# A token, attention and mixture kernel: the halves of q and k spread over the partitions through DRAM instead of by 0/1 products, four hidden buffers for two, a new order for every engine

## The chip, the core and the metric

The kernel runs on one core of one Trainium2 chip. Its five engines each work through a queue of their own in order: TensorE (PE, matrix products), VectorE (DVE), ScalarE (ACT), GpSimd (POOL) and SyncE (SP, which here issues every DMA). They meet through semaphores: an instruction waits until a count is reached, and whatever stands behind it in that queue waits too. The metric is the time on the device in microseconds, lower is better. Time before: a median of 4962.4 us over 3 runs (4959.22 to 4967.59).

## The reference, cut to what matters

```python
# x: (64, 256, 80).  After a 5-tap projection: h: (64, 252, 128)
h = tok(x)                                            # taps, relu, norm over batch and time
h = h + softmax_attention(_layernorm(h))              # 8 heads of 16; a band of +0.1 on the scores
h = h + top2_mixture(_layernorm(h))                   # 8 experts of 256, gelu
h = h + linear_attention(_layernorm(h))               # 8 heads of 16, elu + 1, causal; values of 64
h = h + causal_block(_layernorm(h))                   # 2 heads of 64, then 8 experts of 512, gelu

# softmax_attention:
scores = jnp.einsum('bqhd,bkhd->bhqk', q, k) / np.sqrt(hd) + band
attn = jax.nn.softmax(scores, axis=-1)
# linear_attention:  Q = elu(x @ W_q.T) + 1,  K = elu(x @ W_k.T) + 1
# num = Q . cumsum(K V),  out = num / (Q . cumsum(K))
```

## The kernel before

The 64 sequences are taken in 32 pairs. A pair is 4 tiles of 126 positions, 504 columns (`TOK`). A first phase, up to about 165 us, does the token projection of all pairs and puts it in DRAM (`y_scratch`); the rest goes through the pairs.

To keep near float32 with 16-bit products, each operand is a high and a low half in f16 and a product is three (`mm3`, L1274 to L1276): high with high, high with low, low with high.

Each pair passes through five streams. `softmax_queries_and_keys` (letter q) makes q and k of the softmax attention; `softmax_attention` (a) is that attention and its gates; `linear_and_causal_attention` (l) is the linear attention, the causal attention and the gates of the second mixture; `hidden` (h) is one chunk of 128 hidden columns of an expert, and `output` (o) its way back. In round r the engines work at l of pair r, a of pair r+1, q of pair r+2, and 48 chunks of h and of o. A generator per stream yields its steps, and a string of letters per engine (`PE_ROUND`, `DVE_ROUND`, `ACT_ROUND`, `POOL_ROUND`, L165 to L172) says which stream's next step stands next in that engine's queue. SP has no such string before: it waits for a pair's end, stores it and loads the input of the pair four later.

A chunk of h: PE makes three products of 504 columns into PSUM (`pf`), ACT applies gelu (L838) into one of `HIDS = 2` buffers `hid`, DVE casts the high half (L1239), POOL subtracts for the low half (L615). ACT may write a `hid` buffer again only when POOL has read it. A chunk of o: PE makes 4 x 3 products of 128 columns, and DVE adds at an expert's last chunk (L1258).

The scores of a head have 16 rows for contraction. Both attentions put high and low terms of q and k under each other: 64 partitions per head hold q = (high, high, low, -) against k = (high, low, high, -), so that one product gives the three. In the softmax attention a fourth row carries minus the row maximum in q, against a 1 in k. Getting rows from `qk_hi`/`qk_lo` (128 partitions: head x 16) to the spread layout (`q_spread`, `k_spread`: four groups of two heads) is the work that the change is about. Before, PE does it by products with 0/1 matrices: `spread_queries` (L1329, L1330) and `spread_keys` (L1341, L1342), 2 products of 504 columns per group, 4 groups, for q and k and in both attentions; DVE copies the q groups out of PSUM (L942), ACT the k groups (L680, with the 1 added as a bias). Only 3 (softmax) or 2 (linear) PSUM banks are there, so PE waits for the copies in between.

## Time and profile before

| | us |
|---|---|
| median of 3 runs | 4962.4 |
| lowest, highest | 4959.22, 4967.59 |
| the profiled execution's own time | 4962.4 |
| its span, first to last instruction | 4960.7 |
| PE busy | 4458.9 (90%) |
| DVE busy | 3778.6 (76%) |
| ACT busy | 2839.1 (57%) |
| POOL busy | 2494.6 (50%) |
| mean granted TensorE clock | 0.964 |
| DMA queue of the program | 38.01 MB, 2.7% of 16 engines |

Busy time is the time in which an engine has an instruction at work. Products on PE overlap: the end of one is modelled, and the next begins before it. So a sum over busy times of PE is not the time that its queue needs; the distance between the starts of rows is. A row of the time line gives start, duration, engine, line, operation, the tile written and those read, how often it follows itself, and in brackets the idle time of the engine before it and what ended that. `pa` are the PSUM banks of the attentions, `pf` those of the mixtures.

### The profile page before, as it was taken

Reading aid. Unit: us, or ns where it says so; the run is one execution under the profiler, and the core shown is the slowest. Engines: PE = TensorE matmul, PEld = TensorE weight load, DVE = VectorE, ACT = ScalarE, POOL = GpSimd, SP = SyncE. Lnnn points to the kernel's source line nnn. Section 1 sums busy time; section 2 is a strip of 40 time slices with the busy share of each in tenths; the row PEclk is TensorE's granted clock in tenths of the full one; section 3 lists DMA queues with packets and bytes.
Section 4 is the critical chain, followed back from the end, with each engine's and each line's share of the span. In section 5 each row is a group of like instructions: output and inputs, shape, how many; then the busy total and the mean of one; then the engine's idle time right before and its main releaser. Section 6 shows DMA issues by size and latency. Waiting matters only on the chain.

```text
span 4960.7 us, 106933 instructions
## 1 busy us (share of the span) xinstructions
PE 4458.9 (90%) x42560; PEld 3182.8 (64%) x42560; DVE 3778.6 (76%) x9518; ACT 2839.1 (57%) x4601; POOL 2494.6 (50%) x2392
## 2 busy tenths in 40 slices
PE   7677999999999999999999999999999999999986
PEld 3345766666666666666766666676666666666665
DVE  3356877788877788788788778878778888777864
ACT  3224655666566656656655666565566656655643
POOL 1123555555555555555555555555555555555544
PEclk9778999999999999999999999999999999999998
DMA  4100000000000000000000000000000000000000
GB/s 144 37 3 1 6 6 6 1 6 6 5 6 6 6 1 6 5 6 6 6 6 6 2 6 6 6 6 6 6 1 6 6 6 6 6 6 4 2 3 5
DMA packets 45604, 44.86 MB, mean 9 GB/s; under 512 B 19625, under 2 KB 44081, under 8 KB 45105
## 3 DMA queue, kind: packets, MB, share of 16 engines
q1 hardware_dynamic: 45104, 38.01, 2.7%
q8 instruction: 337, 5.52, 0.5%
q14 instruction: 163, 1.33, 0.1%
HBM read 21.48 MB, written 16.52 MB: 8 GB/s over the span
## 4 chain that ended last, share of the span: by engine, by line
PE 46%; DVE 35%; ACT 9%; POOL 5%; issue 4%; DMA 1%; SPq 0%; ACTq 0%; DVEq 0%
PE pa L1562 7%; PE pf L1274 6%; PE pf L1275 6%; PE pf L1276 6%; DVE hid_hi L1239 5%; DVE xn L931 5%; DVE h L1258 4%; PE pa L1442 3%; ACT hid L838 2%; PE pa L1544 2%; PE pa L1274 2%; PE pa L1428 2%; DVE q_spread L942 2%; DVE minus_max L1037 2%; PE pa L1318 2%
## 5 line engine op out<-in xcount | busy, mean ns | idle before, releaser
L615 POOL TENSOR_TENSOR hid_lo<-hid,hid_hi 128x504 f16<-128x504 f32 x1536 | 1773.5, 1159 | 1890.6 <-DVE hid_hi L1239 1890.6
L838 ACT ACTIVATE hid<-pf,vec 128x504 f32<-128x504 f32 x1536 | 1037.4, 682 | 1103.1 <-POOL hid_lo L615 629.9
L1274 PE MATMUL pf<-w_hi,hid_hi 128*126 128x128 f16 x6144 | 1144.2, 225 | 21.8 <-DVE h L1258 21.8
L1276 PE MATMUL pf<-w_hi,hid_lo 128*126 128x128 f16 x6144 | 1133.0, 223 | 0.0
L1275 PE MATMUL pf<-w_lo,hid_hi 128*126 128x128 f16 x6144 | 1132.9, 223 | 0.0
L1239 DVE CAST hid_hi<-hid 128x504 f16<-128x504 f32 x1536 | 784.2, 517 | 276.6 <-ACT hid L838 275.7
L1274 PEld LDWEIGHTS pf<-w_hi,hid_hi 128*126 128x126 f16 x6144 | 857.0, 139 | 118.9 <-DVE h L1258 33.2
L1275 PEld LDWEIGHTS pf<-w_lo,hid_hi 128*126 128x126 f16 x6144 | 858.0, 140 | 38.4 <-issue 5.1
L1276 PEld LDWEIGHTS pf<-w_hi,hid_lo 128*126 128x126 f16 x6144 | 858.8, 140 | 0.0
L1258 DVE SCALAR_TENSOR_TENSOR h<-pf,gates,h 126x128 f32<-126x128 f32 x2048 | 573.7, 342 | 129.3 <-PE pf L1276 129.1
L1274 PE MATMUL pf<-xf_hi,w_hi 128*128 128x504 f16 x1536 | 602.4, 392 | 18.5 <-ACT hid L838 18.3
L1275 PE MATMUL pf<-xf_lo,w_hi 128*128 128x504 f16 x1536 | 598.1, 389 | 0.0
L1276 PE MATMUL pf<-xf_hi,w_lo 128*128 128x504 f16 x1536 | 596.0, 388 | 0.0
L571 POOL TENSOR_TENSOR pt<-pt,band 126x262 f32<-126x262 f32 x512 | 350.7, 706 | 245.6 <-ACT pt L728 245.5
L1562 PE MATMUL pa<-v,pt 126*126 126x65 f32 x3072 | 399.4, 281 | 1.6 <-DVE o L1139 1.6
L1562 PEld LDWEIGHTS pa<-v,pt 126*126 126x126 f32 x3072 | 367.6, 194 | 23.2 <-issue 8.0
L1037 DVE TENSOR_REDUCE minus_max<-pa 126x2 f16<-126x504 f32 x512 | 321.8, 681 | 52.8 <-PE pa L1405 51.4
L728 ACT ACTIVATE pt<-pa 126x504 f32<-126x504 f32 x512 | 274.5, 588 | 134.5 <-PE pa L1428 133.5
L838 ACT ACT_TABLE_LOAD x248 | 318.2, 1283 | 4.8 <-POOL hid_lo L615 0.4
L1276 PEld LDWEIGHTS pf<-xf_hi,w_lo 128*128 128x128 f16 x1536 | 154.2, 100 | 190.6 <-issue 23.3
L1274 PEld LDWEIGHTS pf<-xf_hi,w_hi 128*128 128x128 f16 x1536 | 159.5, 104 | 134.8 <-ACT hid L838 59.8
L1149 DVE TENSOR_TENSOR pt<-pa,causal 126x504 f32<-126x504 f32 x256 | 173.9, 679 | 92.0 <-PE pa L1544 92.0
(214 smaller groups left out, 8511.5 us busy)
## 6 DMA issues: line engine op xcount, KB each, us to landing
y_scratch<-hid SPq DMA_DIRECT2D x32, 252.0 KB, 2.1
y_in<-y_scratch SPq DMA_DIRECT2D x32, 252.0 KB, 2.8
out<-h SPq DMA_DIRECT2D x64, 126.0 KB
pt<-in_x SPq DMA_DIRECT2D x64, 80.0 KB, 2.5
v<-in_weights SPq DMA_DIRECT2D x4, 953.0 KB, 4.9
o<-in_weights SPq DMA_DIRECT2D x4, 953.0 KB, 5.1
rows<-in_rows SPq DMA_DIRECT2D x1, 136.0 KB
vec<-in_vectors SPq DMA_DIRECT2D x1, 29.0 KB
```

What stands on the lines that cost most here:

```text
L571: nc.gpsimd.tensor_tensor(strip, strip, band[0:TILE], ALU.mult).then_inc(S0["p_band"], 1)
L615: nc.gpsimd.tensor_tensor(hid_lo[:, c % 8], hid[:, c % HIDS], hid_hi[:, c % 8], ALU.subtract).then_inc(hid_lo_done[c % 2], 1)
L728: nc.scalar.activation(pt[0][0:TILE, i % 8], pa0[0:TILE, i % 2, 0:TOK], ACT.Exp, scale=HEAD ** -0.5).then_inc(S0["p_exp"], 1)
L838: nc.scalar.activation(hid[:, c % HIDS], pf[:, c % 2, 0:TOK], func, bias=vec[:, bias:bias + 1]).then_inc(F["hid_ready"], 1)
L931: last = nc.vector.tensor_scalar(xn[a][0:TILE, i], h[0:TILE, i], mv[a][0:TILE, i, 0:1], rstd[a][0:TILE, i:i + 1], ALU.subtract, ALU.mult)
L1037: nc.vector.tensor_reduce(minus_max[0:TILE, 2 * b:2 * b + 2, hd // 2, 64 * (hd % 2) + 48], pa0[0:TILE, i % 3, 0:TOK].rearrange("p (t k) -> ...
L1239: nc.vector.tensor_copy(hid_hi[:, c % 8], hid[:, c % HIDS]).then_inc(F["hid_hi_done"], 1)
L1258: last = nc.vector.scalar_tensor_tensor(h[0:TILE, i], pf[0:TILE, 2, i * D:(i + 1) * D], gates[0:TILE, kind, i, e:e + 1], h[0:TILE, i], ALU ...
L1274: nc.tensor.matmul(out, ah, bh, start=start, stop=False, skip_group_check=skip)
L1275: nc.tensor.matmul(out, ah, bl, start=False, stop=False, skip_group_check=skip)
L1276: return nc.tensor.matmul(out, al, bh, start=False, stop=stop, skip_group_check=skip)
L1562: last = nc.tensor.matmul(pa1[0:TILE, 1, first:first + wide], factors[:, cols(blk)], v1[0:TILE, 2 * b + kt, hd], start=(t == 0), stop=(t = ...
```

## The change

- The 0/1 matrices, `spread_queries` and `spread_keys` go from PE, DVE and ACT. In their place SP stores `qk_hi` and `qk_lo` to a DRAM tensor (`terms`) and loads them back with a stride over the partitions: term 0, 1, 2 of each row go to partitions 4d, 4d+1, 4d+2 of one buffer `qk_spread` that holds q and k. The row of the maximum is now row 3 of each 64 (`MAX_ROW`), and is set back to zero by a small copy from the linear attention's buffer. PE waits on the loads' semaphore before its first product of scores.
- SP gets a string and generators of its own (`SP_ROUND`); the input of a pair is loaded one pair ahead, not four.
- `HIDS` is 4: four `hid` buffers.
- The tables of the top-2 ranks lie in `ob`, the buffer of the softmax attention's output, and no longer in `ts0`, which the causal attention also uses.
- The strings of all engines are new; q has 7 steps for 9, l has 48 for 49.

```diff
-HIDS = 2
+HIDS = 4
-QK_STEPS, A0_STEPS, A1_STEPS = 9, 32, 49
+QK_STEPS, A0_STEPS, A1_STEPS = 7, 32, 48
+TERMS, MAX_ROW = 4, 3
+Q_LO, Q_HI, K_HI, K_LO = range(4)
+SPREAD0, SPREAD1 = 6 * 16, 5 * 16
...
-PE_ROUND = ("lhhaooolhlhoalolhholaholhaohalalhalhaloohahhaloallaahoaloaloalooalhohaalolhalhhloaohlhohlaolooaa"
+PE_ROUND = ("hloolaohohlhaolhhollohalaoahlhahoahalooalohhalhallaalaoohooallhaloohllalhhlahahhaloahohlaaohaloo"
...
+            def store_high(a):
+                dst = term_dram[a][Q_HI:K_HI + 1].rearrange("s p t -> p s t")
+                sp.dma_start(dst, qk_hi[a][:]).then_inc(terms_hi_sent[a], 16)
+            def store_low(a):
+                dst = term_dram[a][Q_LO:K_LO + 1:K_LO - Q_LO].rearrange("s p t -> p s t")
+                sp.dma_start(dst, qk_lo[a][:]).then_inc(terms_lo_sent[a], 16)
+            def load_term(a, row, j, slot, slots=1):
+                src = term_dram[a][slot:slot + slots].rearrange("s (g r) t -> r (s g) t", g=GROUPS)
+                dst = qk16[a][row:128:TERMS, j:j + slots].rearrange("r s g t -> r (s g) t")
+                sp.dma_start(dst, src).then_inc(spread_sent[a], 16)
+            def load_terms(a, p):
+                sp.wait_ge(terms_hi_sent[a], n.plain((p + 1) * 16))
+                load_term(a, 0, 0, Q_HI, 2)
+                load_term(a, 1, 0, Q_HI)
+                load_term(a, 2, 1, K_HI)
+                sp.wait_ge(terms_lo_sent[a], n.plain((p + 1) * 16))
+                load_term(a, 1, 1, K_LO)
+                load_term(a, 2, 0, Q_LO)
...
+                sp.wait_ge(S0["qk_hi_ready"], n(p * 2 + 2))
+                store_high(0)
+                sp.wait_ge(S0["qk_lo_ready"], n(p * 2 + 2))
+                store_low(0)
+                sp.dma_start(q16[0][MAX_ROW:128:64], q16[1][MAX_ROW:128:64]).then_inc(spread_sent[0], 16)
+                load_terms(0, p)
...
-            def spread_keys(a, p):
-                for g in range(GROUPS):
-                    bank = (GROUPS + g) % (3, 2)[a]
-                    act.wait_ge(SS[a]["spread"], n(p * 8 + GROUPS + g + 1))
-                    nc.scalar.activation(k16[a][:, g], pa[a][:, bank, 0:TOK], ACT.Identity,
-                                         bias=one_row[:, 0:1]).then_inc(SS[a]["k_spread"], 1)
...
-            def spread_queries(a, p):
-                for g in range(GROUPS):
-                    dve.wait_ge(SS[a]["spread"], n(p * 8 + g + 1))
-                    nc.vector.tensor_copy(q16[a][:, g], pa[a][:, g % (3, 2)[a], 0:TOK]).then_inc(SS[a]["q_spread"], 1)
...
             def softmax_attention(p):
-                pe.wait_ge(S0["k_spread"], n(p * 4 + 4))
+                pe.wait_ge(spread_sent[0], n.plain((p + 1) * SPREAD0))
+                pe.wait_ge(S0["v_ready"], n(p + 1))
...
                 pe.wait_ge(S1["v1_ready"], n(p * 4 + 4))
-                pe.wait_ge(S1["el_lo"], n(p * 2 + 2))
-                spread_queries(1, p)
-                yield
-                spread_keys(1, p)
-                yield
-                pe.wait_ge(S1["k_spread"], n(p * 4 + 4))
+                pe.wait_ge(spread_sent[1], n.plain((p + 1) * SPREAD1))
```

The order, at three places of a round. First PE in the linear attention, from the end of the last value tile (`pa<-w_hi,xt_lo`) to the first product of its scores (`pa<-q_spread,k_spread`, 126x126). Before:

```order
L1276 MATMUL pa<-w_hi,xt_lo 126x512
L1329 MATMUL pa<-qk_hi,pick_q_hi 128x504
L1330 MATMUL pa<-qk_lo,pick_q_lo 128x504
...
L1405 MATMUL pa<-k_spread,q_spread 126x252 x4
L1341 MATMUL pa<-qk_hi,pick_k_hi 128x504
L1342 MATMUL pa<-qk_lo,pick_k_lo 128x504
...
L1274 MATMUL pf<-xf_hi,w_hi 128x504
L1275 MATMUL pf<-xf_lo,w_hi 128x504
L1276 MATMUL pf<-xf_hi,w_lo 128x504
L1405 MATMUL pa<-k_spread,q_spread 126x252 x4
L1544 MATMUL pa<-q_spread,k_spread 126x126 x4
```

and in the change (`qk_spread` is the one buffer of q and k; 126x252 are the softmax attention's scores, 126x126 the linear one's):

```order
L1306 MATMUL pa<-w_hi,xt_lo 126x512
L1304 MATMUL pf<-xf_hi,w_hi 128x504
L1305 MATMUL pf<-xf_lo,w_hi 128x504
L1306 MATMUL pf<-xf_hi,w_lo 128x504
L1411 MATMUL pa<-qk_spread 126x252 x4
...
L1306 MATMUL pf<-w_hi,hid_lo 126x128
L1411 MATMUL pa<-qk_spread 126x252 x4
L1304 MATMUL pf<-xf_hi,w_hi 128x504
L1305 MATMUL pf<-xf_lo,w_hi 128x504
L1306 MATMUL pf<-xf_hi,w_lo 128x504
L1411 MATMUL pa<-qk_spread 126x252 x4
L1544 MATMUL pa<-qk_spread 126x126 x4
```

The 16 products of the spreading are gone; three chunks of h, one of o and three steps of the softmax attention stand between the last value tile and the scores, and the wait for the loads is at the last row.

Second ACT, from the copies of the linear attention's value tiles (`v<-pa`) to its first copy of scores (`pt<-pa`). Before:

```order
L768 COPY v<-pa 126x8x64
L838 ACTIVATE hid<-pf,vec 128x504 x2
L768 COPY v<-pa 126x8x64 x3
L838 ACTIVATE hid<-pf,vec 128x504
L680 ACTIVATE k_spread<-pa,one_row 128x504 x4
L838 ACTIVATE hid<-pf,vec 128x504
L779 COPY pt<-pa 126x504
```

and in the change:

```order
L809 COPY v<-pa 126x8x64 x3
L877 ACTIVATE hid<-pf,vec 128x504 x3
L809 COPY v<-pa 126x8x64
L877 ACTIVATE hid<-pf,vec 128x504
L818 COPY pt<-pa 126x504
```

The four copies of k are gone and three chunks of h run together.

Third SP. Before, a round has the store of a pair and the load of an input:

```order
L476 DMA out<-h 126x2x128 x2
L468 DMA y_in<-y_scratch 128x504
L476 DMA out<-h 126x2x128 x2
L468 DMA y_in<-y_scratch 128x504
L476 DMA out<-h 126x2x128 x2
```

and in the change, one round (`terms` is the DRAM tensor):

```order
L472 DMA y_in<-y_scratch 128x504
L484 DMA terms<-qk_hi 128x2x504
L488 DMA terms<-qk_lo 128x2x504
L494 DMA qk_spread<-terms 32x8x504
L494 DMA qk_spread<-terms 32x4x504 x4
L480 DMA out<-h 126x2x128 x2
L484 DMA terms<-qk_hi 128x2x504
L488 DMA terms<-qk_lo 128x2x504
L512 DMA qk_spread<-qk_spread 2x2016
L494 DMA qk_spread<-terms 32x8x504
L494 DMA qk_spread<-terms 32x4x504 x4
```

Fifteen DMAs are new in a round: seven for the linear attention, then eight for the softmax attention of the round after.

## Rows read from the trace of the kernel before

**Rows 1.** The page, busy time of each engine.

```profile
PE 4458.9 (90%) x42560; PEld 3182.8 (64%) x42560; DVE 3778.6 (76%) x9518; ACT 2839.1 (57%) x4601; POOL 2494.6 (50%) x2392
```

**Rows 2.** One round in a window: length, busy time (count) by engine, clock, DMA.

```profile
2003.50:2146.10 142.60, 132.10 (x1313) 96.01 (x1312) 116.34 (x296) 87.41 (x142) 77.47 (x74) 0.99 0.02 5
```

**Rows 3.** The page, chain that ended last, share of the span by engine.

```profile
PE 46%; DVE 35%; ACT 9%; POOL 5%; issue 4%; DMA 1%; SPq 0%; ACTq 0%; DVEq 0%
```

**Rows 4.** PE's time line, the linear attention's spreading: start, duration, what, idle before.

```profile
2066.75 0.38 PE L1276 MATMUL pa<-w_hi,xt_lo 128*126 128x512 f16 x1
2067.86 0.39 PE L1329 MATMUL pa<-qk_hi,pick_q_hi 128*128 128x504 f16 x1 [0.73 <-ACT v L768]
...
2070.36 0.43 PE L1405 MATMUL pa<-k_spread,q_spread 64*126 64x252 f16 x4
2070.72 0.39 PE L1341 MATMUL pa<-qk_hi,pick_k_hi 128*128 128x504 f16 x1
...
2072.09 0.39 PE L1341 MATMUL pa<-qk_hi,pick_k_hi 128*128 128x504 f16 x1 [0.29 <-ACT k_spread L680]
...
2073.10 0.38 PE L1274 MATMUL pf<-xf_hi,w_hi 128*128 128x504 f16 x1
```

**Rows 5.** PE's time line, the softmax attention's projections and spreading.

```profile
2034.02 0.38 PE L1274 MATMUL pf<-xf_hi,w_hi 128*128 128x504 f16 x1
...
2038.00 0.38 PE L1329 MATMUL pa<-qk_hi,pick_q_hi 128*128 128x504 f16 x1
...
2039.84 0.38 PE L1274 MATMUL pf<-xf_hi,w_hi 128*128 128x504 f16 x1
...
2041.11 0.22 PE L1274 MATMUL pf<-w_hi,hid_hi 128*126 128x128 f16 x1
...
2041.80 0.60 PE L1355 MATMUL pa<-ident,gates 126*8 126x126 f32 x4
...
2043.06 1.14 PE L1362 MATMUL pa<-b,gate_t 8*126 8x128 f32 x8
2044.13 0.39 PE L1341 MATMUL pa<-qk_hi,pick_k_hi 128*128 128x504 f16 x1
...
2045.93 0.38 PE L1274 MATMUL pf<-xf_hi,w_hi 128*128 128x504 f16 x1
```

**Rows 6.** Groups by line: count, busy us, mean ns of one, idle before and releaser.

```profile
L1341 PE MATMUL pa<-qk_hi,pick_k_hi 128*128 128x504 f16 x256 | 98.2, 384 | 9.4 <-ACT k_spread L680 9.2 <-DVE q_spread L942 0.2
...
L1342 PE MATMUL pa<-qk_lo,pick_k_lo 128*128 128x504 f16 x256 | 96.3, 376 | 0.0
...
L942 DVE CAST q_spread<-pa 128x504 f16<-128x504 f32 x256 | 159.8, 674 | 12.4 <-PE pa L1330 8.8
...
L680 ACT ACTIVATE k_spread<-pa,one_row 128x504 f16<-128x504 f32 x256 | 156.7, 679 | 129.0 <-PE pa L1342 125.1
...
L838 ACT ACT_TABLE_LOAD x248 | 318.2, 1283 | 4.8 <-POOL hid_lo L615 0.4
...
L838 ACT ACTIVATE hid<-pf,vec 128x504 f32<-128x504 f32 x1536 | 1037.4, 682 | 1103.1 <-POOL hid_lo L615 629.9 <-PE pf L1276 464.9
```

**Rows 7.** DVE's time line, the last low half of k in either attention.

```profile
2034.27 0.73 DVE L1017 SCALAR_TENSOR_TENSOR qk_lo<-pa,vec,qk_hi 128x504 f16<-128x504 f32 x1
...
2062.41 0.68 DVE L1116 TENSOR_TENSOR qk_lo<-fs,qk_hi 128x504 f16<-128x504 f32 x1
```

**Rows 8.** PE's time line, the linear attention's second value tile.

```profile
2061.87 0.43 PE L1274 MATMUL pa<-w_hi,xt_hi 128*126 128x512 f16 x1 [0.88 <-DVE fs L1111]
```

**Rows 9.** DMA issues: count, KB each, median us from issue to landing.

```profile
y_scratch<-hid SPq DMA_DIRECT2D x32, 252.0 KB, 2.1
y_in<-y_scratch SPq DMA_DIRECT2D x32, 252.0 KB, 2.8
...
o<-in_weights SPq DMA_DIRECT2D x4, 953.0 KB, 5.1
```

**Rows 10.** SP's queue: start and duration of an issue.

```profile
2146.95 0.45 SPq L468 DMA_DIRECT2D y_in<-y_scratch  x1
```

More of the change, by code:

```diff
@@ L264, in program @@
     y_dram = nc.dram_tensor("y_scratch", (PAIRS, 128, TOK), F32, kind="Internal").ap()
+    term_dram = [nc.dram_tensor(f"terms{i}", (4, 128, TOK), F16, kind="Internal").ap() for i in range(2)]
     with ExitStack() as ctx:
@@ L354, in program @@
         pa = (pa0, pa1)
+        q16, k16 = [x[:, 0] for x in qk16], [x[:, 1] for x in qk16]
         TURN = 1
@@ new lines, in load_terms, with softmax_queries_and_keys @@
+            def load_terms(a, p):
[6 more added lines that the diff above has]
+                load_term(a, 2, 0, Q_LO)
+            def softmax_queries_and_keys(p):
+                for _ in range(6):
+                    yield
+                sp.wait_ge(S0["qk_hi_ready"], n(p * 2 + 2))
[4 more added lines that the diff above has]
+                load_terms(0, p)
+                yield
@@ new lines, in softmax_attention, with linear_and_causal_attention @@
+            def softmax_attention(p):
+                if isinstance(p, Count) or p + 1 < PAIRS:
+                    load_y(p + 1)
+                for _ in range(A0_STEPS):
+                    yield
+            def linear_and_causal_attention(p):
+                for _ in range(4):
+                    yield
+                sp.wait_ge(S1["el_hi"], n(p * 2 + 2))
+                store_high(1)
+                sp.wait_ge(S1["el_lo"], n(p * 2 + 2))
+                store_low(1)
+                load_terms(1, p)
+                for _ in range(A1_STEPS - 4):
+                    yield
@@ L487, in _, with hidden, output @@
+            def hidden(kind, p, c):
+                pass
+            def output(kind, p, j):
+                if kind == 1 and j == EXPERTS * CHUNKS1 - 1:
+                    store_out(p)
+            load_y(0)
+            sp.wait_ge(consts_built, 1)
+            run_rounds(softmax_queries_and_keys, softmax_attention, linear_and_causal_attention, hidden, output, n,
+                       SP_ROUND)
             sp.wait_ge(out_sent, 32 * PAIRS)
@@ L554, in softmax_queries_and_keys @@
                 norm(0, p * 2)
-                for _ in range(6):
+                for _ in range(4):
                     yield
@@ L594, in linear_and_causal_attention @@
                 nc.gpsimd.memset(v1[0:TILE, :, :, LIN_VALUE:LIN_VALUE + 1], 1.0).then_inc(S1["v1_ones"], 1)
-                for _ in range(25):
+                for _ in range(24):
                     yield
```

101 lines of the change are left out of this document (26 added, 75 removed).

## The prediction, made before the changed kernel was run

> **What bounds the kernel now.** I read the page's busy times first, then one round in a window, then the chain of waits, then PE's time line at the two places where the spreading stands. PE is busy 90% of the span, the next engine, DVE, 76% [rows 1]. After the token phase the time is a row of equal rounds: one takes 142.6 us, with PE busy 132.1, DVE 116.3, ACT 87.4 and POOL 77.5, at a clock of 0.99 [rows 2]. So PE idles 10.5 us of a round. The chain that ended last runs 46% over PE and 35% over DVE [rows 3]: PE's queue is the longest, but the chain leaves it for the norms and casts of DVE. A microsecond taken out of PE's queue should be worth most of a microsecond, not all of it.
>
> **The spreading taken away.** In each attention 4 groups x 2 products for q and the same for k, so 32 products a round; the orders agree, PE's queue has 1023 rows fewer. What they occupy is read from the distance of starts. Softmax: q from 2038.00 to 2039.84, k from 2044.13 to 2045.93, 1.84 + 1.80 = 3.64 us [rows 5], nearly without a wait (16 products at 0.23). Linear: the last value product starts at 2066.75 and is followed at about +0.21, so the stretch runs from 2066.96 to 2073.10, less 0.36 for a step of the softmax attention in the middle (2070.36 to 2070.72): 5.78 us [rows 4]. Here PE waits for copies, 0.73 for the values and 0.29 for k in the rows shown. Together 9.42 us a round; some 31 rounds' worth, with the first and last pair partly alone, give 292 us.
>
> By busy times the four groups, 96.3 to 98.2 us each [rows 6], would be 390 us. That is too much, since a row's 0.38 us covers a product whose successor starts 0.21 later. The Trainium skill (Perfetto Trace Analysis, Identifying the Most-Contended Engine) says the same of matmul busy time, that pipelining makes it a bad measure, and offers instead matmul work and weight-load busy time; by that alone the products would be worth less than 292, since it leaves out the waits between them.
>
> DVE loses 256 casts of 0.674 us, 160 us in all or 5.0 us a round; ACT loses 256 of 0.679 us, 157 us or 4.9 a round [rows 6]. They lie beside PE's work but in the chain of the linear attention, so I count nothing extra for them; they are what lets DVE follow (116.3 - 5.0 = 111.3 in a shorter round).
>
> **The round trip added.** No row shows it; I bound it by other DMAs. An issue holds SP 0.45 us, some 0.47 with what is between [rows 10]. A store of 252 KB to DRAM lands 2.1 us after issue, a load of 252 KB after 2.8, one of 953 KB after 5.1 [rows 9]. The new stores have 252 KB, the loads 252 or 126 KB. Take t = 0 when the last low half of k is ready; the high half is ready 0.7 earlier. High store issued at -0.65, landed at 1.45. Low store issued at 0.05, landed at 2.15; the small copy fits before 1.45. Three loads of high terms are issued from 1.45 to 2.85, the two low ones at 2.85 and 3.32; the last lands at 3.32 + 2.8 = 6.1. The upper bound takes 5.1 for each landing: high landed at 4.45, last issue at 6.3, ready at 11.4. The lower bound takes 2.1: 1.45 + 1.87 + 2.1 = 5.4. I take 6.1, since the sizes are those of the 252 KB rows.
>
> The Trainium skill (DMA: Bandwidth & Descriptors, Anatomy of one DMA) speaks against this change: about 2.0 us fixed per DMA plus its bytes at 436 GB/s, and a completion that can be surprisingly late when the target is HBM. The formula would make 2.6 for a store and 2.3 for a short load, estimates that leave the 6.1 us where it is; the warning on HBM isn't borne out by the trace, where the store (2.1) lands sooner than the load (2.8).
>
> Does PE get there first? The wait stops all of PE's queue, h and o included. A chunk of h takes 0.64 (two from 2039.84 to 2041.11), one of o 0.69 (2041.11 to 2041.80) [rows 5], a step of softmax scores 0.36 [rows 4].
> - Linear: the low half of k is ready at 2062.41 + 0.68 = 2063.09 [rows 7], so the terms at 2069.2. PE starts the second value tile at 2061.87 [rows 8]; in the new order it then has 3 value tiles (1.94), 5 steps of scores (1.80), 2 of o (1.38) and 4 of h (2.54), and gets to the wait at 2069.5. Slack 0.3.
> - Softmax: PE ends the projections at 2034.02 [rows 5], the low half of k is there at 2035.00 [rows 7], the terms at 2041.1. PE has 6 of o (4.14), 3 of h (1.91), a gate turn (0.60) and the gate bias (1.07) [rows 5] before its wait: 2041.7. Slack 0.6.
> Both just fit. As any unevenness turns into a wait, I charge 0.35 us each: 0.7 a round, 22 us. Bounds: 0, and 5.3 more per attention less the slack, 9.7 a round, 301 us. SP itself has 15 new issues a round, 7 us of 143; queued behind its waits are the input of the next pair and the output, both needed half a round later.
>
> **The rest.** Four `hid` buffers for two: ACT waits 629.9 us for POOL to free one [rows 6], but ACT has 55 us free in a round and PE's queue hardly feels it; I take 0, bounds 0 and a gain of half of PE's other idle time, (10.5 - 2.1)/2 = 4.2 a round (2.1 lies in the spreading), 130 us. The new strings: ACT gets 525 table loads for 465, 60 x 1.283 = 77 us more on an engine with room [rows 6]; I take 0, bounds -77 and +77, since the order may also put them better. The ranks in `ob`: no operation and no wait changes, 0. The first phase: constants on POOL are other ones, beside the token phase; 0. The first pair's spreading, alone, swaps some 8 us for 6; 0.
>
> Sum: -292 + 22 = -270 on the profiled execution, whose own time of 4962.4 equals the median. 4692, say 4695 us; a round of about 134 us.
>
> **The rivals.**
> 1. DVE takes over. With PE shorter, the chain sits on DVE's norms and casts (35% already, [rows 3]), and a round gives only what DVE loses, 5.0 us: 155 us, 4807. For: PE waits for `xn` and the scores wait for the maxima. Against: DVE idles 26 of 143 us.
> 2. The new order and four buffers work better than the old ones on top: 270 + 130, 4560. For: 629.9 us of waits for POOL. Against: they hardly reach PE.
> 3. The extra table loads fall on the path, 2 a round at 1.283: 4695 + 77 = 4772. For: gelu and exp alternate, and 8 heads' exps sit in the chain of the softmax attention. Against: ACT has 39% free.
> 4. The round trip lands late. At 5.1 us per landing both waits come 5.3 later, less slack 0.9: +9.7 a round against -9.4, so 4962 + 10 = 4972, and slower the longer it is; it decides from 5.0 us per landing. Place: PE's first product of scores in each attention. For: rows of 1008 bytes with a stride over the partitions, five loads at once, each behind the other. Against: 252 KB in 2.1 and 2.8. The skill's same page (Latency and other measured facts) has HBM access at 0.2 us on average and 2 us at high load; the load here is 5 GB/s [rows 2], and the change makes it some 15.
> That the change doesn't do what it says is out: the products are gone from the order.
>
> **How the numbers follow.** Forecast 0.58 (own range 4640 to 4750), rival 1 0.16, rival 2 0.12, rival 3 0.06, rival 4 0.08 (three quarters of it slower by over 0.2%, a quarter within). The range reaches from half of rival 2, 4590, over rivals 3 and 1 to 4840; some 0.06 lie below and 0.12 above. A measurement of this kernel tells 0.2%, about 10 us, from no change. Faster 0.91, same 0.03, slower 0.06.
>
> **What would show it.** A round of 134 us between stores of the output, PE busy near 125 in it; the first scores of each attention waiting for the DMA 0 to 1 us; landings of 2 to 3 us; 60 more table loads and no longer path for it. Wrong, if PE's wait for the terms is over 2 us a round (then rival 4's step), if DVE's idle time falls under 18 us a round (rival 1), or if PE idles under 5 us a round (rival 2).

## The result, and the profile after

The changed kernel takes 4452.2 us (median of 4 runs, 4444.95 to 4458.42) against 4962.9 us for the kernel before in the same comparison: a ratio of 0.897, 95% interval 0.8954 to 0.8986. The forecast was 4695 us, its range ended at 4590. The sign was right, the size was not: the gain is 511 us, and 270 were forecast.

The page's busy times, which answer to [rows 1]:

```profile
PE 4152.4 (93%) x41536; PEld 3069.8 (69%) x41536; DVE 3435.9 (77%) x9262; ACT 2749.9 (62%) x4405; POOL 2573.4 (58%) x2365
```

One round, from one store of the output to the next. The columns are those of [rows 2]: length, then busy time and count of PE, PEld, DVE, ACT and POOL, the granted clock, DMA share, GB/s.

```profile
1957.30:2082.90 125.60, 122.33 (x1282) 92.22 (x1281) 105.15 (x289) 84.96 (x136) 79.90 (x74) 1.00 0.09 26
```

A round went from 142.6 to 125.6 us. (These are single rounds, and short ones. The means of all rounds between 850 and 4000 us are 143.6 us, 11.0 of it idle on PE, and 126.3, 3.8 of it idle.) PE's busy time fell by 9.8 us, which the removal of the products accounts for. PE's idle time fell from 10.5 to 3.3 us, and that the forecast did not have. The chain by engine, against [rows 3]:

```profile
PE 52%; DVE 25%; ACT 7%; DMA 6%; POOL 3%; issue 3%; SPq 2%; ACTq 0%; DVEq 0%
```

DVE's share fell from 35% to 25%. The waits of PE show where (us in total, times, longest). After:

```profile
PE pf L1304 <- DVE h L1288: 41.1, 49, 5.5
PE pa L1348 <- DVE xn L970: 37.1, 36, 4.6
PE pa L1411 <- DMA qk_spread<-terms: 31.7, 26, 8.2
...
PE pa L1544 <- DMA qk_spread<-terms: 13.3, 10, 6.0
...
PE pa L1364 <- DVE gates L1023: 4.0, 1, 4.0
```

The same view of the kernel before:

```profile
PE pa L1318 <- DVE xn L931: 115.7, 66, 4.5
PE pa L1355 <- DVE gates L989: 54.2, 32, 4.0
...
PE pa L1329 <- ACT v L768: 23.5, 32, 0.7
```

PE's waits for the norms (`xn`) went from 115.7 to 37.1 us, those for the gates of the softmax attention (L989 before, L1023 now) from 54.2 to 4.0. The new wait, for the terms, is 31.7 + 13.3 = 45.0 us, 1.4 a round.

The DMAs that the change adds, without the small copy of the maximum's row, against [rows 9]:

```profile
qk_spread<-terms SPq DMA_DIRECT2D x256, 126.0 KB, 2.8
terms<-qk_hi SPq DMA_DIRECT2D x64, 252.0 KB, 2.4
terms<-qk_lo SPq DMA_DIRECT2D x64, 252.0 KB, 2.6
qk_spread<-terms SPq DMA_DIRECT2D x64, 252.0 KB, 3.0
```

SP's queue in one linear attention (start, us, engine, line, DMA, how many in a row), against [rows 10]:

```profile
2006.55 0.37 SPq L484 DMA_DIRECT2D terms<-qk_hi  x1
2007.27 0.36 SPq L488 DMA_DIRECT2D terms<-qk_lo  x1
2009.10 3.18 SPq L494 DMA_DIRECT2D qk_spread<-terms  x5
```

Five loads take 3.18 us to issue, 0.64 each. ACT's rows, against [rows 6]:

```profile
L877 ACT ACTIVATE hid<-pf,vec 128x504 f32<-128x504 f32 x1536 | 1018.0, 681 | 716.6 <-PE pf L1306 611.4 <-POOL hid_lo L666 94.1
...
L877 ACT ACT_TABLE_LOAD x278 | 356.7, 1283 | 4.9
```

ACT's waits for POOL to free a `hid` buffer went from 629.9 to 94.1 us; the table loads rose by 60, as the order said. And DVE's norms, which do the same work on the same shapes, are shorter. After, then before:

```profile
L970 DVE TENSOR_SCALAR xn<-ha,mv,rstd 126x128 f32<-126x128 f32 x256 | 74.1, 351 | 19.6 <-POOL rstd L598 19.6
L970 DVE TENSOR_SCALAR xn<-h,mv,rstd 126x128 f32<-126x128 f32 x256 | 72.8, 348 | 22.6 <-POOL rstd L598 22.2
```

```profile
L931 DVE TENSOR_SCALAR xn<-h,mv,rstd 126x128 f32<-126x128 f32 x256 | 170.1, 734 | 23.8 <-POOL rstd L547 21.6
...
L931 DVE TENSOR_SCALAR xn<-ha,mv,rstd 126x128 f32<-126x128 f32 x256 | 94.0, 429 | 2.3 <-POOL rstd L547 2.3
```

### The profile page after: what moved, and what is told of

Same layout as the page of the kernel before. It is cut to its first block, busy times and chain, and to the rows that moved or that the text cites. A ratio compares the mean times of both kernels' runs of the same rounds, so it can differ in the third digit from the quotient of the medians.

```text
span 4450.2 us, 104889 instructions
## 1 busy us (share of the span) xinstructions
PE 4152.4 (93%) x41536; PEld 3069.8 (69%) x41536; DVE 3435.9 (77%) x9262; ACT 2749.9 (62%) x4405; POOL 2573.4 (58%) x2365
## 3 DMA queue, kind: packets, MB, share of 16 engines
q14 instruction: 160, 1.31, 0.1%
## 4 chain that ended last, share of the span: by engine, by line
PE 52%; DVE 25%; ACT 7%; DMA 6%; POOL 3%; issue 3%; SPq 2%; ACTq 0%; DVEq 0%
PE pa L1562 9%; PE pf L1304 8%; PE pf L1306 7%; PE pf L1305 7%; DVE minus_max L1069 4%; PE pa L1448 3%; DMA qk_spread<-terms 3%; DVE h L1288 2%; PE pa L1544 2%; PE pa L1348 2%; POOL inv_norm L656 2%; PE pa L1434 2%; DVE hid_hi L1269 2%; SPq L494 2%; DMA terms<-qk_hi 2%
## 5 line engine op out<-in xcount | busy, mean ns | idle before, releaser
L666 POOL TENSOR_TENSOR hid_lo<-hid,hid_hi 128x504 f16<-128x504 f32 x1536 | 1855.1, 1223 | 1478.2 <-DVE hid_hi L1269 1477.0
L877 ACT ACTIVATE hid<-pf,vec 128x504 f32<-128x504 f32 x1536 | 1018.0, 681 | 716.6 <-PE pf L1306 611.4
L1306 PE MATMUL pf<-w_hi,hid_lo 128*126 128x128 f16 x6144 | 1118.7, 222 | 0.0
L1305 PE MATMUL pf<-w_lo,hid_hi 128*126 128x128 f16 x6144 | 1118.3, 222 | 0.0
L1269 DVE CAST hid_hi<-hid 128x504 f16<-128x504 f32 x1536 | 760.1, 521 | 118.9 <-ACT hid L877 115.3
L1304 PE MATMUL pf<-xf_hi,w_hi 128*128 128x504 f16 x1536 | 586.4, 382 | 0.1
L1305 PE MATMUL pf<-xf_lo,w_hi 128*128 128x504 f16 x1536 | 581.5, 379 | 0.0
L1306 PE MATMUL pf<-xf_hi,w_lo 128*128 128x504 f16 x1536 | 581.3, 378 | 0.0
L1160 DVE TENSOR_SCALAR den<-pa 126x4 f32<-126x4 f32 x256 | 41.1, 161 | 357.0 <-PE pa L1562 357.0
L724 ACT ACTIVATE ot_hi<-pa 128x504 f16<-128x504 f32 x192 | 113.0, 589 | 189.0 <-PE pa L1348 188.9
```

What stands on the lines that cost most here:

```text
L666: nc.gpsimd.tensor_tensor(hid_lo[:, c % 8], hid[:, c % HIDS], hid_hi[:, c % 8], ALU.subtract).then_inc(hid_lo_done[c % 2], 1)
L877: nc.scalar.activation(hid[:, c % HIDS], pf[:, c % 2, 0:TOK], func, bias=vec[:, bias:bias + 1]).then_inc(F["hid_ready"], 1)
L1269: nc.vector.tensor_copy(hid_hi[:, c % 8], hid[:, c % HIDS]).then_inc(F["hid_hi_done"], 1)
L1304: nc.tensor.matmul(out, ah, bh, start=start, stop=False, skip_group_check=skip)
L1305: nc.tensor.matmul(out, ah, bl, start=False, stop=False, skip_group_check=skip)
L1306: return nc.tensor.matmul(out, al, bh, start=False, stop=stop, skip_group_check=skip)
```

## The experiments

All runs in one table. Each was compared with the kernel before on its own chip (medians of that from 4958 to 4982 us), so the ratios are to be compared; "us" is the ratio's distance from 1 times 4962. A round is one that starts near 2000 us, with PE's busy and idle time in it. Single rounds of one execution differ by 1 to 3 us, some by 5, so sums are taken from whole executions further down. The clock is the mean of the whole profiled execution.

| run | ratio, 95% interval | us | round | PE busy | PE idle | clock |
|---|---|---|---|---|---|---|
| before | 1 | 0 | 142.6 | 132.1 | 10.5 | 0.964 |
| e1 round trip, old order, 2 buffers | 0.9818 (0.979 to 0.9847) | -90 | 139.5 | 125.9 | 13.6 | 0.945 |
| e2 the same, 4 buffers | 0.9764 (0.9729 to 0.98) | -117 | 139.4 | 128.5 | 10.9 | 0.947 |
| e3 products, old order, 4 buffers | 0.9987 (0.9966 to 1.0008) | -6 | 143.5 | 132.1 | 11.4 | 0.962 |
| e4 products, new order, 4 buffers | 0.9658 (0.9631 to 0.9685) | -170 | 138.7 | 132.2 | 6.5 | 0.967 |
| the change | 0.8970 (0.8954 to 0.8986) | -511 | 125.6 | 122.3 | 3.3 | 0.968 |
| e5 before, casts behind norms | 1.0050 (1.0035 to 1.0066) | +25 | 145.5 | 132.2 | 13.3 | 0.968 |
| e6 e2, casts behind norms | 0.9651 (0.9615 to 0.9687) | -173 | 137.1 | 123.8 | 13.4 | 0.960 |
| e7 change, casts ahead of norms | 0.9211 (0.9181 to 0.9241) | -391 | 130.8 | 123.0 | 7.8 | 0.967 |
| e8 change, one cast behind gates | 0.8954 (0.8925 to 0.8984) | -519 | 126.6 | 122.3 | 4.3 | 0.970 |
| e9 e3, casts behind norms | 1.0027 (1.001 to 1.0044) | +13 | 143.7 | 131.9 | 11.9 | 0.964 |
| e10 change, four more stores | 0.9678 (0.9659 to 0.9697) | -160 | 137.9 | 126.6 | 11.3 | 0.935 |
| e11 change, terms early | 0.8932 (0.8918 to 0.8946) | -530 | 126.3 | 122.8 | 3.5 | 0.974 |
| e12 change, POOL's old string | 0.9827 (0.9813 to 0.9842) | -86 | 140.6 | 128.6 | 12.0 | 0.927 |
| e13 e12, five steps earlier | 0.9211 (0.9193 to 0.9228) | -391 | 131.2 | 123.2 | 8.1 | 0.963 |
| e14 change, one more store | 0.9127 (0.9104 to 0.915) | -433 | 130.4 | 124.2 | 6.1 | 0.962 |

### The parts apart: e1 to e4

e1 and e2 are the changed kernel with the four strings of before, less the two last q and the last l:

```diff
-QK_STEPS, A0_STEPS, A1_STEPS = 9, 32, 49
+QK_STEPS, A0_STEPS, A1_STEPS = 7, 32, 48
-HIDS = 4
+HIDS = 2
```

(the second pair of lines in e1 alone). e3 and e4 go the other way: the kernel before with `HIDS = 4`, and for e4 with the new strings, the ranks in `ob`, and the products at the place where the change has its wait. To make room for the buffers, one 0/1 matrix stands for all four. So low halves and keys are spread by the wrong rows; the instructions and their sizes stay:

```diff
-        pick_q_lo = sb("pick_q_lo", [128, GROUPS, 128], F16)
-        pick_k_hi = sb("pick_k_hi", [128, GROUPS, 128], F16)
-        pick_k_lo = sb("pick_k_lo", [128, GROUPS, 128], F16)
+        pick_q_lo = pick_k_hi = pick_k_lo = pick_q_hi
```

e1, what was expected:

> The changed kernel with the old strings of all engines (less the steps q8, q9 and l9 that the spreading had) and two hid buffers: the DRAM round trip alone. The prediction's step, 9.42 us a round less 0.7 of waits: about 4690 us (4660 to 4730). Rival, the spreading is worth more than its length in PE's queue because DVE and ACT lose 5 us each too: 4560 or less. Rival, it is worth little without the new order: over 4800.

e2:

> As the first, with four hid buffers. If the buffers bring the missing 240 us by themselves: 4450 to 4550. If the order does, which only may use them: within 0.5% of the first, near 4690.

e3:

> The kernel before with four hid buffers and nothing else; for room one 0/1 matrix stands for all four, so that low halves and keys are spread by the wrong rows, with the same instructions. Buffers theory: 4720 to 4800. Order theory: 4940 to 4965, no change.

e4:

> The kernel before with the new strings, four buffers and the ranks in ob, but with the spreading by products, put at the start of the steps where the change waits for its loads (one 0/1 matrix for all four, as in the third). Order theory: order and buffers bring 240 us here too, and the spreading costs 9.4 us a round or somewhat more, as q and k stand together: 4720 to 4800. Rival, the new order works only because the spreading is gone: 4900 or more.

What follows. e1 fell where the round trip is worth little without the new order (over 4800 us), e3 where the order theory had it; e4, at 4809 us, just missed the 4720 to 4800 of that theory. The round trip is worth 90 us alone and 111 with four buffers in the old order (e3 to e2), but 341 in the new one (e4 to the change). The strings are worth 163 us with the products (e3 to e4) and 394 with the round trip (e2 to the change). The buffers by themselves give nothing with the products (e3) and 27 us with the round trip, at intervals that still overlap. Added up, e2 and the strings with products would give 280 us; the change gives 511. So about 230 us belong to neither part but to both together.

The new strings with two buffers weren't run, so what the four buffers are worth in the new order isn't known. In the trace of the change ACT starts 1061 of its 1536 chunks before POOL has read the chunk two back (540 in e2); with two buffers it would have to wait there.

Whole profiled executions (us) show where PE's time went. Idle is the span less PE's busy time:

| | span | PE busy | PE idle |
|---|---|---|---|
| e3 products, old order, 4 buffers | 4961.8 | 4460.1 | 501.7 |
| e2 round trip, old order, 4 buffers | 4860.1 | 4304.6 | 555.5 |
| e4 products, new order, 4 buffers | 4808.8 | 4442.8 | 366.0 |
| the change | 4450.2 | 4152.4 | 297.8 |

In the new order, from e4 to the change, PE is busy for 290.4 us less and idle for 68.2 less. The waits that go with the products are those for the copies between them:

```profile
PE pa L1322 <- DVE q_spread L937: 50.6, 33, 1.6
...
PE pa L1397 <- ACT k_spread L678: 29.3, 32, 0.9
PE pa L1533 <- ACT k_spread L678: 24.7, 32, 0.8
```

That is 104.6 us, or 3.3 a round, and 9.1 more in two smaller rows of the same kind. The change has 45.0 us of waits for the terms in their place: 113.7 - 45.0 = 68.7, which is the 68.2 of idle time.

In the old order, from e3 to e2, the same products go. But PE's busy time falls by 155.5 us only, and its idle time rises by 53.8. e2 and the change have the same 41536 instructions on PE; they take 4304.6 us busy in e2 and 4152.4 in the change. By these spans 256.9 us belong to both parts together: 122.0 are PE's waits, and 134.9 are the same instructions keeping PE busy for longer, at a lower clock (0.947 for 0.968). e2's waits:

```profile
PE pa L1348 <- DVE xn L970: 149.4, 65, 4.6
PE pa L1364 <- DVE gates L1023: 55.5, 31, 4.0
```

The norms were late already in e3 (137.4 us), and stayed so. New in e2 are waits for the terms (22.9 + 14.4 us), for the gates of the second mixture (26.6, in e3 5.1) and for the copy of the turned gates on ACT (16.3, in e3 1.8). The clock of the run is 0.947, 0.962 in e3. What a stop does to the clock is shown below, by e12.

### Casts and norms on DVE: e5, e6, e9, e7, e8

The norms of one shape took 734 ns in one order and 348 in the other. DVE's time line of before shows four of them in 2.77 us:

```profile
2049.35 2.77 DVE L931 TENSOR_SCALAR xn<-h,mv,rstd 126x128 f32<-126x128 f32 x4 [0.57 <-POOL rstd L547]
```

and POOL's, at the same time, two low halves of the casts that DVE had made just ahead of the norms:

```profile
2049.29 2.23 POOL L615 TENSOR_TENSOR hid_lo<-hid,hid_hi 128x504 f16<-128x504 f32 x2
```

In the changed kernel four norms, of which only the first meets the last 0.3 us of a low half, take 1.15 us:

```profile
2106.68 1.15 DVE L970 TENSOR_SCALAR xn<-ha,mv,rstd 126x128 f32<-126x128 f32 x4
```

One by one, the first two of the four in before take 1.16 and 1.26 us, and end within 0.2 us of the end of a low half; the other two take 0.34. So a norm stands still for most of the time in which POOL's low half (1.1 us) is at work. The Trainium skill (SBUF — State Buffer, Terms) has the mechanism: DVE and GpSimd share a pair of ports, held for a whole instruction, and the loser blocks fully instead of sharing. By that rule a collision costs the rest of the other instruction, and the trace agrees roughly: 2.77 - 1.15 = 1.6 us lost beside two low halves of 1.1. The mean of 734 ns is a mixture of the two kinds.

e5 takes seven casts of hidden chunks from ahead of the norms to behind them, in DVE's string alone; e6 is that edit on e2 and e9 on e3:

```diff
-DVE_ROUND = ("olhoholahloalhlhhlhoooalaohalhalaooallohhaahalaallaaohlhlloaooolhhlllahaaoaohlohoohhloahlhaoalol"
-          "ahhololhahlaolhloaahaooaohloohqalhaohlohololllholohhqqqholoqhlhlohqohlohlqohlolhqllhhholoq")
+DVE_ROUND = ("oloolhhahloalhllhhhoooalaohalhalaooallohhaahalaallaaohlhlloaooolhhlllahaaoaohlohoohhloahlhaoa"
+          "lolahhololhalhaolhloaaahooaohloohqalhaohlohololllholohhqqqoloqhhlhlohqohlohlqohlolhqllhhholoq")
```

> The kernel before; in DVE's string alone seven of the 48 h stand right behind a step that works on SBUF in float32 (the norms l2, l29, q5, the elu step l6, the ranks a29) and no longer right ahead of it, so that POOL has no low half to make while the step runs. Collision theory: the norm rows fall from 734 ns to about 290, DVE is 4 to 7 us a round less busy, and as PE waits for xn and for the gates, the time falls by 60 to 200 us. Rival, the durations follow from something else (where h lies, the size of the order's change): rows of 734 ns stay, time within 0.5%.

The norms did get short, 444 and 344 ns, and DVE's busy time fell from 3778.6 to 3624.9 us. The kernel became 0.5% slower, where 60 to 200 us less were expected. ACT's row offers a reason, which e9 below takes away again:

```profile
L838 ACT ACTIVATE hid<-pf,vec 128x504 f32<-128x504 f32 x1536 | 1037.4, 682 | 1243.1 <-POOL hid_lo L615 890.3 <-PE pf L1276 345.5 <-issue 0.2
```

ACT waits 890.3 us for POOL, 629.9 before: a later cast makes a later low half. With four buffers and the round trip:

> The second kernel (round trip, old strings, four buffers, 4859 us) with the same edit of DVE's string. If the chain over DVE held back the gain of the round trip, the edit is worth more here than in the kernel before: 150 to 350 us. If the old strings hold it back elsewhere: as in the fifth or less.

e6 gives 56 us over e2, a third to a sixth of what was expected. With four buffers and the products, which was to tell whether the buffers had spoiled e5:

> The kernel before (products with 0/1 matrices, old strings), with four hidden buffers (one 0/1 matrix serves for all four products, which leaves memory for them; it changes the values) and with seven casts of hidden chunks moved behind DVE's norms. With two buffers the same move cost 0.5% although DVE's norms became 290 ns shorter. Theory (a collision of DVE and POOL is paid for in the path, and with two buffers the gain was eaten by ACT, which waited longer for the later casts): with four buffers the move gives what it gave with the DRAM round trip, 0.965 / 0.976 = 0.989, so 0.988 of the time before, some 4905 us. Rival (with the products in PE's queue the norms don't set the time at all, and the buffers have nothing to do with it): 0.998 as without the move, 4955 to 4970.

They had not: with four buffers ACT waits 0.6 us for POOL, and the time is still 1.0027, 0.4% above e3. The norms took 444 and 346 ns, PE's wait for them fell from 137.4 to 63.9 us, that for the gates from 62.6 to 6.6, and other waits rose in their place (in e3 they are 37.2, 20.9, 1.4 and 0 us, in the order of the rows without `xn`):

```profile
PE pa L1602 <- DVE v L1186: 73.8, 32, 9.3
PE pa L1316 <- DVE xn L929: 63.9, 37, 4.6
PE pf L1272 <- DVE h L1256: 56.3, 49, 1.9
PE pa L1272 <- DVE xt_lo L935: 42.7, 31, 1.4
PE pf L1272 <- POOL hid_lo L613: 41.0, 29, 1.4
```

One of these rows is new, PE's wait for POOL's low half: the casts put behind the norms are themselves what POOL, and then PE, wait for. That this is the reason for the other rows too isn't shown. Now the other direction, in the changed kernel: the h letters just ahead of l2, l28, q5 and a29 instead of behind (l2) or a step or two before (the others). The edit moves four h; the text below says five.

```diff
-DVE_ROUND = ("looalhoollhoahlhlaaohhoaoalhaalhhlaaaolooohhllaaalohlholalohohlaahlllhlaaoohhohalhaholhhoaalooao"
-          "lohhlahlalooaohqolhlhaoalhhoohhaoalolhloololoqqqhholhlllalohohlholqlolhhqoolhhqohhhlool")
+DVE_ROUND = ("looahloollhoahlhlaaohhoaoalhaalhhlaaaolooohhllaaalohlholalohohlaahlllhlaaoohhohalhaholhhoaa"
+          "looaolohhlalahlooaohqolhlaohalhhoohhaoalolhloololoqqqhholhlllalohohlolhqlolhhqoolhhqohhhlool")
```

> The changed kernel; in DVE's string five h move from behind to right ahead of l2, l28, q5 and a29 (l6 has one already). Collision theory: xn rows back to 600 ns and more, DVE 3 to 5 us a round busier, time up by 60 to 150 us. Rival, the new order has room for it: within 0.5% of 4452.

0.0241 above the change, 120 us, for DVE's norms at 443 and 440 ns and PE's wait for them at 127.8 instead of 37.1 us. The norms did not reach the 600 ns that were expected, and together they are only 47 us longer. DVE's row has a second cost of the same size, which is no collision:

```profile
L970 DVE TENSOR_SCALAR xn<-h,mv,rstd 126x128 f32<-126x128 f32 x256 | 97.5, 443 | 70.2 <-POOL rstd L598 70.2
```

DVE idles 70.2 us ahead of these norms, 22.6 in the change, until POOL has made `rstd`. By these rows about half of the 91 us that PE waits longer is longer norms, and half is norms that start later, since POOL gets to `rstd` behind the low half. Where little else is late, the place of a few casts decides over 120 us; where other things are late, an edit of the same kind, in the other direction, gives 56 (e6), costs 20 (e3 to e9) or costs 25 (e5). In e8 one h went from ahead of a28 to behind a29, to free the gates, which stand at 1241 ns in the change against 192 in the kernel before:

```diff
-          "lohhlahlalooaohqolhlhaoalhhoohhaoalolhloololoqqqhholhlllalohohlholqlolhhqoolhhqohhhlool")
+          "looaolohhlahlalooaohqolhlaoahlhhoohhaoalolhloololoqqqhholhlllalohohlholqlolhhqoolhhqohhhlool")
```

> The changed kernel with one h moved from ahead of a28 to behind a29, the only place in its string where a row is still hit (1.31 us for the gates, 0.70 for the probabilities, against 0.19 each). Collision theory: 1 to 1.6 us a round less on DVE, on the way to the gate turn: 4400 to 4440. Rival, the gate chain has slack: 4450.

It missed: the gates stayed at 1240 ns, and the time is that of the change. The trace of e8 shows why. What runs beside the gates is not a low half but another of POOL's instructions, which the place of a cast on DVE did not move away:

```profile
2073.34 1.96 POOL L652 TENSOR_TENSOR o<-v 126x1024 f32<-126x1024 f32 x1 [1.56 <-ACT v L829]
2074.03 1.31 DVE L1023 SCALAR_TENSOR_TENSOR gates<-lge,lg 126x32 f32<-126x32 f32 x1
```

This instruction lies over the gates in 30 of 32 pairs in e8 and in the change, and in none in the kernel before. PE hardly waits for the gates in either (4.0 us), so a fix would likely have given nothing.

### How late the terms may come: e10, e14, e11

```diff
                 sp.dma_start(dst, qk_hi[a][:]).then_inc(terms_hi_sent[a], 16)
+                for i in range(4):
+                    dst = spare_dram[i].rearrange("s p t -> p s t")
+                    sp.dma_start(dst, qk_hi[a][:]).then_inc(terms_hi_sent[a], 16)
...
-                sp.wait_ge(terms_hi_sent[a], n.plain((p + 1) * 16))
+                sp.wait_ge(terms_hi_sent[a], n.plain((p + 1) * 80))
```

> The changed kernel with four more stores of the high halves, to DRAM that nobody reads, ahead of the low store in SP's queue; the loads of the terms wait for them. Five issues of some 0.45 us stand where one stood, so the terms come 1.8 us later in each attention (2 to 2.5 if the stores get into each other's way). Theory (the round trip just fits, PE's slack at the wait is near zero and what it waits now is 1.4 us a round): all but a few tenths of it is paid: 2 x 1.5 x 31, so 75 to 115 us more, ratio 0.912 to 0.920. Rival (the terms come in time with room to spare, and the 45 us of waits in the profile are waits for other things that came last): under 25 us more, ratio below 0.902.

In the time line of SP the loads start 6.37 us after the first store in one linear attention (2.55 in the change). Over all 32 the means are 6.4 for 2.5 us in the linear and 6.6 for 2.6 in the softmax attention: 3.9 and 4.0 later. The issues of the stores take part of that, and the added stores land after 3.7 us, the low one after 4.1 (2.6 in the change). PE's waits for the terms:

```profile
PE pa L1415 <- DMA qk_spread<-terms: 158.1, 32, 11.7
PE pa L1548 <- DMA qk_spread<-terms: 118.6, 32, 9.7
```

276.7 us for 45.0: 232 more, 4.0 per softmax attention of the 4.0 and 3.3 per linear one of the 3.9. So the slack was near nothing, as the theory had it. But the kernel is 351 us longer, where 75 to 115 were expected, and one and a half times the added waits: in the profiled executions PE idles 223 us more and is busy 123 us more. One wait in windows on PE (stretch, its length, PE busy, clock, DMA share, GB/s):

```profile
2021.02:2024.33 3.31, 0.01 (x1) 0.89 0.66 196
2024.33:2029.00 4.67, 4.67 (x41) 0.50 0.02 4
2029.00:2034.00 5.00, 5.00 (x44) 0.86 0.00 0
```

PE stands still for 3.31 us, and then works for 4.67 us at half clock (1.2 for 2.4 GHz) and for 5 more at 0.86: 4.67 x 0.50 + 5.00 x 0.14 = 3.0 us of work lost. The stop costs 6.3 us.

e14 has one more store instead of four (`range(1)`, and 32 for 80):

> As the run with four more stores (0.968), with one more store of the high halves instead of four: the loads start 0.8 to 1.2 us later in each attention instead of 3.8 and 4.8. With four, PE's waits for the terms grew by 232 us and the time by 344, at a clock of 0.935 for 0.968. Theory A (each us in which PE stands still costs 1.5, since the clock falls with it): waits for the terms 35 to 60 us longer in sum, time 50 to 90 us longer, ratio 0.908 to 0.916, clock near 0.96. Theory B (only the long stops of 2 us and more are followed by the low clock): the waits grow as much, the time by no more than they, 35 to 60 us, ratio 0.904 to 0.909, and the clock stays at 0.965 to 0.97.

PE's waits for the terms are 78.8 + 34.9 = 113.7 us, 69 more; the ratio says 78 us, the profiled execution alone 98, at a clock of 0.962. Theory A asked for 50 to 90 at a clock near 0.96 and B for no more than the waits at 0.965 or more. It leans to A. By the profiled executions, in which the waits were read, the factor is 98 for 69 or 1.4 (PE idles 64 us more and is busy 34 more); by the ratios it is 78 for 69 or 1.1. The two kernels did not run side by side (the kernel before took 4981.8 us beside e14 and 4962.9 beside the change), and the factor for short stops stays open.

e11 leaves the stores out and loads fixed data, as soon as the high half is ready; the small copy now stands behind the loads:

```diff
-                src = term_dram[a][slot:slot + slots].rearrange("s (g r) t -> r (s g) t", g=GROUPS)
+                src = fixed_dram[slot:slot + slots].rearrange("s (g r) t -> r (s g) t", g=GROUPS)
...
-                sp.wait_ge(terms_hi_sent[a], n.plain((p + 1) * 16))
...
-                sp.wait_ge(terms_lo_sent[a], n.plain((p + 1) * 16))
```

> The changed kernel with the round trip's first half left out: no stores, and the five loads of each attention take fixed data from DRAM as soon as the high half of k is ready. The computation on q and k is not that of the reference. The terms come some 1.5 to 2.5 us earlier. Theory (45 us of PE's waits, 1.4 a round, are the price of the round trip): 30 to 45 us less, ratio 0.888 to 0.891. Rival (when these waits go, PE waits for something else at the same place, the norms or the maxima): under 10 us less, ratio 0.895 to 0.897.

19 us by the ratios, 30 by the two profiled spans (4420.3 for 4450.2), between the two theories. PE's waits for these loads and the small copy are 3.5 + 6.9 us instead of 45.0. So the round trip's whole lateness is worth 0.4 to 0.7% of the changed kernel's time; there is no more to be had there.

### One string put back: e12 and e13

e12 is the change with POOL's string of before and all others new:

> The changed kernel with POOL's string of before (less its two last q and last l step, to have the new number of steps); all the other engines keep the new strings. It tells which part of the 406 us of the new order lies with POOL. Theory (the new order pays by the place of DVE's casts and norms and of PE's steps; POOL only has to be in time, and the four buffers cover it): 0 to 60 us more, ratio 0.897 to 0.909, and DVE's norms collide more often. Rival (the order of POOL's low halves and norms is what lets PE run on): 150 us or more, ratio above 0.927.

0.9827: 425 of the 511 us are lost, far more than the 0 to 60 of the theory and on the rival's side. PE's waits:

```profile
PE pa L1448 <- POOL pt L622: 155.3, 35, 5.1
PE pa L1348 <- DVE xn L970: 118.6, 66, 4.6
```

and one of the first kind in windows on PE:

```profile
2184.00:2189.10 5.10, 5.10 (x51) 1.00 0.00 0
2189.10:2194.18 5.08, 0.01 (x2) 0.90 0.01 2
2194.18:2199.00 4.82, 4.82 (x33) 0.50 0.01 3
2199.00:2204.00 5.00, 5.00 (x39) 0.56 0.00 2
2204.00:2209.00 5.00, 5.00 (x67) 1.00 0.00 0
```

A stop of 5.07 us, 9.8 us at half clock or little more, 4.82 x 0.50 + 5.00 x 0.44 = 4.6 us of work lost: 9.7 us for one late step, about 310 us over 32 pairs. What PE waits for is the first four products with the band, which POOL has behind a low half that comes late:

```profile
2190.38 1.14 POOL L666 TENSOR_TENSOR hid_lo<-hid,hid_hi 128x504 f16<-128x504 f32 x1 [3.38 <-DVE hid_hi L1269]
2191.48 3.95 POOL L622 TENSOR_TENSOR pt<-pt,band 126x262 f32<-126x262 f32 x6
```

POOL idles 3.38 us in front of the low half that stands ahead of the band. e13 moves five letters of POOL's string and nothing else (a7 to a11, up past one or two h and the l and o between):

```diff
-POOL_ROUND = ("lhlhlhoolalolhhaaholoaolahlhhlaohhlllaolahlaaalaahooahaaolaohlhhlhaaoaoooohhlaooohhlaalllhl"
+POOL_ROUND = ("lhlhlhoolalolhhaaholoaolahlhhlaohaaaaahlllolhllaahooahaaolaohlhhlhaaoaoooohhlaooohhlaalllhl"
```

> As the run with POOL's string of before in the changed kernel (0.983), but with five steps of the softmax attention in POOL's string (a7 to a11; a10 and a11 are the first four band products) moved up to ahead of the last of two low halves, so that they stand behind the same low half as in the changed kernel. In the run before PE waited 155.3 us for them, 5.07 us at a time, once a round. Theory (one late step made most of the loss, by its wait and by the lower clock behind it): 155 us and half as much again for the clock go, 200 to 250 us less, ratio 0.932 to 0.943, granted clock at 0.95 or more. Rival (with that wait gone PE stops at the next late step, the norms and the collisions with the low halves, since POOL's string as a whole is off): under 80 us less, ratio above 0.966.

0.9211, 306 us less than e12 (275.5 by the profiled spans, from two chips), more than the upper end of the theory and near the 310 of the sum above. PE's wait for the band is 3.1 us (3.2 in the change), PE's busy time fell from 4329.0 to 4197.2 at a clock of 0.963 for 0.927: 152 us of stops and 132 of slow work. The 120 us that are left to the change go with DVE's time: busy 3575.9 for 3435.9, norms at 538 and 565 ns, together 105 us longer, and PE's wait for them 118.5 us instead of 37.1. Here DVE does not idle longer ahead of its norms (21.2 us for 22.6), so this wait is put down to the collisions.

## Why the prediction was wrong, step by step

- **The spreading, -292 us, "read off as distance".** PE's 9.42 us a round were right as an occupancy (e4 to the change: 290.4 us less busy, 9.4 a round; the 2.1 of waits that I had in it is 1.4 by the view of waits, which has 23.5 + 12.2 + 9.2 us). The step that failed is to take it as a gain whatever else stands in the round: it gave 90 us in the old order (e1), 111 from e3 to e2, and 341 in the new. I had written that a microsecond out of PE's queue is worth most of one. In the old order it was worth a third, because PE's waits rose and its clock fell (e3 to e2: 53.8 us more idle, and busy for 155.5 us less instead of 290.4).
- **"The new strings: 0".** This is the step that cost the forecast its place. They gave 163 us with the products and 394 with the round trip. The bounds of 77 both ways came from the count of table loads, which has nothing to do with what the strings change: which dependent step on DVE and POOL is ready when PE gets there. In my rows that quantity was PE's idle time, 10.5 us a round, of which 8.4 were not in the spreading; it was a bound that I used for the buffers (half of it) and not for the strings.
- **Four buffers: 0.** Right in the old order (e3, where ACT's wait for POOL fell to 0.6 us and the time stayed; e1 to e2 is unclear). The 629.9 us of ACT's waits hardly reached PE. What they are worth in the new order wasn't measured.
- **The round trip's wait, +0.7 a round.** 1.4 measured. The terms came later than forecast: I had 0.47 us for an issue and 2.1 for a store's landing, and the rows show 0.64 and 2.4. From the first store to the last load's landing that is about 5.1 + 2.8 = 7.9 us instead of 6.75. The slack near zero was right (e10: 4.0 us of 4.0 and 3.3 of 3.9 paid). The formula of the Trainium skill that the prediction quotes (DMA: Bandwidth & Descriptors, Anatomy of one DMA) was fitted on DMAs that GpSimd issues, while these come from SP; its 2.6 and 2.3 us met 2.4 and 2.6 for the stores and 2.8 for a short load. The traffic of a round is 26 GB/s, where the prediction had some 15; nothing hung on it.
- **Table loads, the ranks: 0.** 525 table loads in all as forecast, in e4 too, which is 163 us faster than e3. So they didn't keep the new order from its gain; no run takes them away alone, and nothing shows them to cost anything.
- **Rival 1 (DVE takes over)** did not happen: DVE idles 20.4 us of a round, above the 18 that I named. **Rival 4 (late terms)** had the right place and the wrong price: it took a wait for its own length, and e10 paid half as much again.
- **Rival 2 (the order and the buffers work better)** is what happened, and the mark I had set for it, PE idle under 5 us a round, came out at 3.3. Its price was too low, 4560 for 4452, and its chance too: it took half of the old idle time as the most, where two thirds went (10.5 to 3.3; 11.0 to 3.8 in the means), and it knew nothing of the clock. That it was named at 0.12 is no merit of the sum, which took order and buffers at nothing.

What is shown and what isn't: that the two parts work together is shown (e1 to e4), that one late step makes PE stop and then run at half clock, and what this costs, too (e10, e12, e13). That the order of DVE's casts, or of POOL's steps, is worth 120 us in the new order is shown by e7 and e13. How much of it is the collisions of DVE and POOL is argued from the rows: in e13 the greater part, in e7 about half. How the 394 us of the strings split over the engines is not settled: of the old strings only POOL's was run beside the other new ones, and e13 prices that one, repaired, at 120 us. The shares of DVE's, ACT's and PE's strings stay open, and so does what the four buffers add in the new order.

## What to carry to other kernels

In a kernel of in-order queues the price of a removed operation and the price of a new order are not two terms to be added: in the old order part of PE's freed time turned into waits for the next late step, and part of it went to a lower clock behind the longer waits. When a change rewrites the order, look first at what the bounding engine waits for (here 10.5 us a round), take all of it as the far end of the gain, and look on each helper engine for the step that stands behind something not yet ready. Before you price a stop of TensorE, look in the windows behind one for the granted clock.

## What the runs showed of the hardware

- A stop of PE can cost more than its length. Behind stops of 5.07 and 3.31 us the clock was 0.50 (1.2 GHz for 2.4) for 4.7 to 4.8 us and 0.56 and 0.86 for the next 5. It need not: in e13 a stop of 2.36 us, PE's wait for `xn`, was followed by the lower clock in one round, and the same stop by the full clock in the next (stretch, its length, PE busy, clock, DMA share, GB/s):

```profile
1990.35:1992.71 2.36, 0.00 (x2) 1.00 0.00 0
1992.71:1997.71 5.00, 5.00 (x37) 0.66 0.01 3
...
2122.14:2124.49 2.35, 0.00 (x1) 1.00 0.00 0
2124.49:2129.49 5.00, 4.22 (x39) 1.00 0.02 5
```

  Over a kernel the factor was 1.5 (e10: 351 us for 232), 2.0 (e12 against e13: 306 for 152) and 1.1 (e14: 78 for 69) by the ratios, and 1.5, 1.8 and 1.4 by the profiled spans. The Trainium skill (TensorE: Matmul & The Clock Gate, HAM oscillation — how this bites in real kernels) tells of the same in a kernel that waits for a DMA ahead of each slice: it starts each slice cold and pays each time. The trace agrees, for waits on POOL and DVE as well.
- DVE's norm of 126x128 in float32 took 348 ns in the mean where hardly any ran beside POOL's subtraction (1.1 us), and 734 where many did; one by one they took 0.34 or about 1.2 us. The gates of 126x32 took 192 ns, or 1.31 us under a POOL instruction of 2 us. Such a row that changes its mean with the order alone is the mark of a collision.
- The issue of a load with a stride over the partitions held SP 0.64 us, that of a store 0.37; of six stores of 252 KB issued in a row (e10) the first landed after 2.4 us, the next four after 3.7 and the last after 4.1.
